# Expert loop and recurrences of a fused two-layer block: third pair of banks, scaled sums, later exponentials

## The reference

```
ek, ekv = exp(min(f, 30)), exp(min(f, 30)) * f
a[t] = a[t-1] * decay + ekv[t]          # forward, and once more from the end backward
b[t] = b[t-1] * decay + ek[t]
euk  = exp(min(u + f, 30))
num  = a_fwd + a_bwd - ekv + euk * f
den  = b_fwd + b_bwd - ek + euk
out  = sigmoid(x) * num / max(den, 1e-8) * (0.8 + 0.2 tf)
layer 0: x = x + MoE(attention(out))    # 16 heads, 8 experts, top 2, FF = 896
layer 1: x = x + fp8_mlp(out')          # weights and rows rounded to e4m3, 704 inner channels
```

## Time and profile before

| | us |
|---|---|
| median of three runs (648.53 to 650.09) | 648.83 |
| the profiled execution | 650.63 |
| its span, first to last instruction | 648.5 |

### The profile page before, as it was taken

The page is one execution under the profiler, slowest core; times in us unless marked ns, Lnnn a source line. Parts: engine busy times, 40 slices in busy tenths (PEclk is TensorE's granted clock), DMA queues, the critical chain, the costliest instruction groups (busy, mean ns, idle before and its releaser), DMA issues.

```text
span 648.5 us, 10885 instructions
## 1 busy us (share of the span) xinstructions
PE 503.3 (78%) x3862; PEld 411.0 (63%) x3862; DVE 518.6 (80%) x973; ACT 359.1 (55%) x760; POOL 262.1 (40%) x212
## 2 busy tenths in 40 slices
PE   2011198599999999998578997979988999666775
PEld 1000043278888878887458896979978999533453
DVE  4999868688888888885528958998889889579993
ACT  3226235687777778775115545645455456447671
POOL 3565114754444445530554279361362140070011
PEclk9999999989999999999579999999998999978797
DMA  8300004050000000000278796779875764030001
GB/s 269 118 0 1 1 1 129 0 172 2 1 2 3 1 2 10 25 1 3 77 252 327 273 312 142 259 269 254 294 285 166 285 147 132 27 103 25 9 25 33
DMA packets 36529, 71.85 MB, mean 111 GB/s; under 512 B 5276, under 2 KB 21916, under 8 KB 36220
## 3 DMA queue, kind: packets, MB, share of 16 engines
q10 hardware_dynamic: 16912, 46.27, 21.0%
q1 hardware_dynamic: 16491, 16.75, 8.1%
q0 software_dynamic: 3072, 8.14, 5.2%
HBM read 66.03 MB, written 5.12 MB: 110 GB/s over the span
## 4 chain that ended last, share of the span: by engine, by line
PE 49%; DVE 32%; issue 7%; ACT 6%; POOL 2%; DMA 1%; ACTq 0%; DVEq 0%; SPq 0%; POOLq 0%; PEldq 0%
PE pw L418 8%; PE pb L418 8%; PE pb L609 7%; PE sc L609 6%; PE sc L459 6%; PE po L418 4%; PE pt L470 3%; DVE areg L1168 2%; DVE areg L1154 2%; DVE areg L1152 2%; DVE rs L1566 1%; DVE areg L1513 1%; DVE areg L1165 1%; DVE areg L1506 1%; DVE breg L1225 1%
## 5 line engine op out<-in xcount | busy, mean ns | idle before, releaser
L609 PE MATMUL pb<-areg,wreg 128*128 128x128 f32 x736 | 86.3, 275 | 6.1 <-DVE areg L1506 3.8
L609 PEld LDWEIGHTS pb<-areg,wreg 128*128 128x128 f32 x736 | 84.0, 192 | 7.2 <-issue 5.2
L609 PE MATMUL sc<-areg,wreg 128*128 128x128 f32 x552 | 67.5, 280 | 8.7 <-DVE areg L1506 8.7
L1711 POOL TENSOR_TENSOR breg<-breg,con 128x512 f32<-128x512 f32 x32 | 40.7, 1271 | 80.9 <-ACT breg L846 80.9
L609 PEld LDWEIGHTS sc<-areg,wreg 128*128 128x128 f32 x552 | 65.3, 196 | 9.5 <-DVE areg L1506 9.5
L418 PE MATMUL pb<-areg,wreg 128*128 128x512 f16 x240 | 58.9, 382 | 2.0 <-ACT breg L846 1.9
L980 ACT CAST areg<-areg 128x512 f16<-128x512 f32 (+1 forms) x46 | 25.8, 561 | 62.5 <-DVE areg L1506 56.0
L418 PE MATMUL pw<-areg 128*128 128x256 f16 x406 | 56.5, 273 | 1.6 <-DVE areg L1520 1.6
L854 ACT ACTIVATE breg<-breg,mx 128x128 f32<-128x128 f32 (+1 forms) x128 | 56.6, 445 | 2.0 <-DVE mx L1276 1.9
L459 PE MATMUL sc<-areg,breg 128*128 128x128 f32 (+1 forms) x256 | 48.0, 331 | 6.4 <-DVE mx L1276 5.2
L1520 DVE TENSOR_TENSOR areg<-areg 128x512 f16<-128x512 f32 (+1 forms) x46 | 39.8, 866 | 14.0 <-ACT areg L980 13.7
(11 more groups left out here) (245 smaller groups left out, 1246.7 us busy)
## 6 DMA issues: line engine op xcount, KB each, us to landing
wreg<-in_L_ffn_w ACTq DMA_DIRECT2D x46, 896.0 KB, 7.3
wreg<-in_L_ffn_w SPq DMA_DIRECT2D x8, 896.0 KB, 7.8
ys_dram<-areg ACTq DMA_DIRECT2D x23, 128.0 KB
wreg<-in_L_ffn_wq SPq DMA_DIRECT2D x1, 2048.0 KB, 8.6
wreg<-in_L_ffn_wo SPq DMA_DIRECT2D x1, 2048.0 KB, 8.1
areg<-in_fside_BxSxS ACTq DMA_DIRECT2D x4, 256.0 KB, 5.5
x_in<-in_x SPq DMA_DIRECT2D x4, 256.0 KB, 4.0
h_dram<-areg SPq DMA_DIRECT2D x8, 128.0 KB, 1.7
```

Source lines behind the costliest of these rows:

```text
L609: last = nc.tensor.matmul(bank[:, j * P:(j + 1) * P], up_w[n % SLOTS_UP][:, m, c, at:at + P], xsT[:, parity, c * P:(c + 1) * P], start=c = ...
L1711: G.tensor_tensor(t2[:, parity, :].rearrange("p (b n) -> p b n", b=2), t2[:, parity, :].rearrange("p (b n) -> p b n", b=2), rope_sin.rearr ...
```

## The change

1. Up products use three pairs of banks in turn, `pb2`, `sc2`, `pt2`: part p of tile n takes pair (2n + p) mod 3 and waits for the product of the part three before.
2. Backward states of the next step, times the decay, are added to the forward states: bwd[t+1] * decay equals bwd[t] less the input of t. So the input need not be subtracted, and GpSimd's subtraction (L1694) goes, with the link before it. The sum becomes two scalar-tensor-tensor instructions, one for each half of the channels.
3. The exponentials of the second recurrence come at tiles 1, 6, 9 and 15, before at 0, 5, 8 and 14.
4. The up weights of tiles 0 to 2 are loaded by SyncE, those of tiles 1 and 2 when the first gather has landed; before, ScalarE issued them, 1 and 2 behind its copy of x of tile 0.
5. VectorE takes the product of part 1 before the low half of part 0.
6. GpSimd's four residual sums are spread: one behind each gather of tiles 18 and 19, two ahead of the first folding.

```diff
+        def load_up(eng, n):
+            k = n % SLOTS_UP
+            if n >= SLOTS_UP:
+                eng.wait_ge(s["upb_done"], n - SLOTS_UP + 1)
+            e = eng.value_load(tmi[0:1, n:n + 1], min_val=0, max_val=NE - 1)
+            for m, name in enumerate(("L0_ffn_w1", "L0_ffn_w3")):
+                eng.dma_start(up_w[k][:, m], t[name][bass.ds(e, 1)].rearrange("e (c p) n -> p (e c) n", p=P)).then_inc(s_u[k], 16)
...
+            sp.wait_ge(s["wo_done"], 2)
+            sp.wait_ge(s["tmi_ready"], 1)
+            load_up(sp, 0)
+            sp.wait_ge(s_xs[0], 16)
+            load_up(sp, 1)
+            load_up(sp, 2)
             sp.wait_ge(s["tmap_ready"], 1)
...
+        def up_pair(n, part):
+            return (pb2, sc2, pt2)[(2 * n + part) % 3]
...
             def up(n, parity, part):
                 first, count = (0, FA // P) if part == 0 else (FA // P, FB // P)
+                before = 2 * n + part - 3
+                if before >= 0:
+                    pe.wait_ge(s["inner_b_done" if before % 2 else "inner_a_done"], before // 2 + 1)
                 for m in range(2):
-                    bank = pb[m] if part == 0 else sc2[:, m]
+                    bank = up_pair(n, part)[:, m, :]
...
-                    if n >= 1:
-                        pe.wait_ge(s["inner_a_done"], n)
                     up(n, parity, 0)
...
-                    if n >= 1:
-                        pe.wait_ge(s["inner_b_done"], n)
                     up(n, parity, 1)
...
-            act.wait_ge(s["wo_done"], 2)
-            act.wait_ge(s["tmi_ready"], 1)
-            load_up(0)
             act.wait_ge(s["tmap_ready"], 1)
             act.wait_ge(s["h2_out"], 16 * NT)
             copy_xT(0, 0)
-            load_up(1)
-            load_up(2)
...
-            exponentials_at = {0: 0, 5: 1, 8: 2, 14: 3}
+            exponentials_at = {1: 0, 6: 1, 9: 2, 15: 3}
...
+            def add_later_states(l, b, fwd, bwd):
+                for c in range(C):
+                    lo, hi = c * S, (c + 1) * S
+                    last = V.scalar_tensor_tensor(fwd[:, :, lo:hi - 1], bwd[:, :, lo + 1:hi], decay[:, l, c, b:b + 1],
+                                                  fwd[:, :, lo:hi - 1], ALU.mult, ALU.add)
+                return last
...
-                link(V.tensor_tensor(fwd[:, :, :], fwd[:, :, :], bwd[:, :, :], ALU.add))
+                link(add_later_states(0, b, fwd, bwd))
...
-                    link(V.tensor_tensor(fwd[:, :, :], fwd[:, :, :], bwd[:, :, :], ALU.add))
+                    link(add_later_states(1, b, fwd, bwd))
...
+                silu(n, 1)
                 inner_low(n, n % 2, 0)
-                silu(n, 1)
                 w2_low(n, n % 2)
...
-                link(G.tensor_tensor(U[:, 0, :], U[:, 1, :], fT[:, b, :], ALU.mult))
-                G.tensor_tensor(U, U, E, ALU.subtract).then_inc(s["u_ready"], 1)
+                G.tensor_tensor(U[:, 0, :], U[:, 1, :], fT[:, b, :], ALU.mult).then_inc(s["u_ready"], 1)
...
             load_scales(0, 2 * INTER)
             gather_tiles(18)
-            for b in range(B):
-                last = G.tensor_tensor(x0[:, TT * b:TT * (b + 1), :].rearrange("p i n -> p (i n)"),
-                                       x0[:, TT * b:TT * (b + 1), :].rearrange("p i n -> p (i n)"), x_in[:, b, :], ALU.add)
-            last.then_inc(s["xsum_ready"], 1)
-            gather_tiles(19, 20)
+            add_residual(0)
+            gather_tiles(19)
+            add_residual(1)
+            gather_tiles(20)
             pool.wait_ge(s["rq_ready"], 3)
             pool.wait_ge(s["rq_copied"], 2)
             pool.wait_ge(s["scale_in"], 16)
+            add_residual(2)
+            add_residual(3).then_inc(s["xsum_ready"], 1)
             fold_scales(0)
```

More of the change, by code:

```diff
@@ L1001, in _ @@
                         act.wait_ge(s["inner_low"], 2 * n - 1)
-                    nc.scalar.activation(inner[:, 0:FA], pb[0][:, :], ACT.Silu).then_inc(s["silu_a_done"], 1)
+                    nc.scalar.activation(inner[:, 0:FA], up_pair(n, 0)[:, 0, :], ACT.Silu).then_inc(s["silu_a_done"], 1)
                 if n + 1 < MT:
@@ L1013, in _ @@
                         act.wait_ge(s["inner_low"], 2 * n)
-                    nc.scalar.activation(inner[:, FA:FF], sc2[:, 0, 0:FB], ACT.Silu).then_inc(s["silu_b_done"], 1)
+                    nc.scalar.activation(inner[:, FA:FF], up_pair(n, 1)[:, 0, 0:FB], ACT.Silu).then_inc(s["silu_b_done"], 1)
                     if n + SLOTS_UP < MT:
-                        load_up(n + SLOTS_UP)
+                        load_up(act, n + SLOTS_UP)
                     inner_high(n, parity, 1)
@@ L1503, in silu @@
                 lo, hi = (0, FA) if part == 0 else (FA, FF)
-                bank = pb[1][:, 0:FA] if part == 0 else sc2[:, 1, 0:FB]
+                bank = up_pair(n, part)[:, 1, 0:hi - lo]
                 dve.wait_ge(s["silu_a_done" if part == 0 else "silu_b_done"], n + 1)
@@ L1780, in _, with add_residual @@
             recurrence_inputs(1, 3)
+            def add_residual(b):
+                return G.tensor_tensor(x0[:, TT * b:TT * (b + 1), :].rearrange("p i n -> p (i n)"),
+                                       x0[:, TT * b:TT * (b + 1), :].rearrange("p i n -> p (i n)"), x_in[:, b, :], ALU.add)
             def load_scales(lo, hi):
```

## The result

| | before | after |
|---|---|---|
| median, us | 649.46 (648.53 to 650.78, 4 runs) | 638.43 (637.43 to 640.37, 4 runs) |
| the profiled execution, us | 650.63 | 639.25 |
| its span, us | 648.5 | 637.4 |
| from the start to the first projection | 86.69 | 82.19 |
| from there to the first up product | 247.77 | 246.69 |

The ratio is 0.984, with a 95% interval of 0.980 to 0.987. The kernel is 11.0 us faster; 20.1 us were forecast, and 638.4 lies outside the range of 624.5 to 636.5. The table of stages says where to look: the first stage gave the 4.5 us that it was to give, the loop gave 5.05 of 15.6, so 10.6 us are missing there.

What follows compares the result with a forecast made beforehand. The expert loop was taken as bound by TensorE, its idle time the prize. First stage 4.5 plus loop 15.6 made 20.1 us less, forecast 628.7 us, own range 625.5 to 631.5, wider range 624.5 to 636.5.

Steps and rivals of the forecast that it cites:

- Part 1: First recurrence: dropping GpSimd's subtraction saves 5.3 us, two scaled sums cost 0.8 us, so 4.5 us less.
- the rival of half the rate: VectorE's scaled sums run at half rate, 2.6 us a pair, 1.2 more in each of four batches: 633 us; chance 0.05.
- on another victim: First stage, batch 0: GpSimd's remaining product still delays some other VectorE instruction, a toll of about 1 us.
- Part 3: Expert loop: three bank pairs and the new order end bank waits, 12.5 us together; rounding gives 1.5, tile 15's clock 1.9.
- Part 2: Loop: later exponentials end SiLU's lateness; tile 8's gather goes out near 395.6, takes 4.0 us, wanted near 401.
- cover of 1.5 us: Tile 8: the forecast margin, some 1.5 us, between the gather's landing and TensorE wanting its rows.
- The fourth rival: GpSimd, waiting longer at the exponentials, sends gathers late at tiles 8, 12, 18; TensorE stands, up to 656 us; chance 0.03.
- The second rival: Banks do nothing: ScalarE's copy of x holds up products as long; 8.7 us of waits stay, 638 us; chance 0.08.
- The end of the loop: Behind the last tile the new order leaves SiLU's lateness unhidden: a loss of 0.4 us.
- Part 4: Loop: GpSimd's split residual sums still hold VectorE somewhat; TensorE loses 0.5 us, bounds 0 to 3.
- Part 5: Tile 1: weight load from SyncE goes out about 1.0 us sooner, VectorE's late rounding eats 0.4, gain 0.6 us.
- The first rival: VectorE becomes the loop's bound and loses 6 us over 14 tiles: 635 us; chance 0.20.

Runs made afterwards that it cites:

- run 8: Changed kernel with the scales sent behind the gathers, plus GpSimd's subtraction and VectorE's plain sum back in both layers: 635.21 us, ratio 0.979.
- run 1: Changed kernel with GpSimd's send of the first scales moved behind the gathers of tiles 8 to 11: 629.34 us, ratio 0.967.
- run 6: Changed kernel with the scales sent behind the gathers, plus the exponentials at their old tiles 0, 5, 8 and 14: 635.50 us, ratio 0.980.
- run 4: Kernel before the change with only the exponentials moved to tiles 1, 6, 9 and 15: 648.37 us, ratio 0.998.
- run 7: Changed kernel with the scales sent behind the gathers, plus up products on two pairs of banks again: 629.70 us, ratio 0.970.
- run 5: Changed kernel with the exponentials at old tiles 0, 5, 8 and 14, the send still ahead of the gathers: 636.79 us, ratio 0.979.
- run 9: Changed kernel with the scales sent behind the gathers, plus VectorE's low half of part 0 ahead of the product of part 1 again: 630.42 us.
- run 11: Changed kernel with the scales sent behind the gathers, plus four residual sums in one row ahead of the gathers of tiles 19 and 20: 626.50 us.
- run 12: Changed kernel with the scales sent behind the gathers, plus two pairs of banks and the residual sums in one row: 627.10 us, ratio 0.966.
- run 3: Changed kernel with the send in its place, but each partition's 8 scales written as one run of 32 bytes: 629.88 us, ratio 0.970.

## Why the prediction failed, point by point

**The bound of the loop** was read rightly: TensorE wherever nothing holds it. It ran tiles 10 to 15 without a break, at 8.96 and 8.76 us a tile.

**Part 1 held.** The forecast was 4.5 us for the first stage and 4.5 came between these two traces. Over all traces the first projection starts at 81.8 us on average with the edit (eleven kernels, 80.9 to 82.5) and at 85.9 without it (three, 85.4 to 86.7): 4.1 us, so the last decimal was luck. VectorE's rows of the first stage, which answer:

```profile
12.34 0.43 DVE L1132 TENSOR_SCALAR areg<-ratio 128x512 f32<-128x512 f32 x1
...
18.96 2.23 DVE L1155 SCALAR_TENSOR_TENSOR areg<-areg,decay 128x510 f32<-128x510 f32 x2
21.22 1.23 DVE L1178 TENSOR_TENSOR areg<-areg 128x1024 f32<-128x1024 f32 x1
...
42.08 0.42 DVE L1132 TENSOR_SCALAR areg<-ratio 128x512 f32<-128x512 f32 x1
...
49.87 1.44 DVE L1155 SCALAR_TENSOR_TENSOR areg<-areg,decay 128x510 f32<-128x510 f32 x2
```

The clamps fell from 2.51 and 2.57 to 0.43 and 0.42 us, the sum with U from 3.26 to 1.23. A pair of scaled sums takes 1.44 us where 1.42 was taken, so the rival of half the rate, and with it the rule of the Trainium skill's Vector Engine (DVE) Microarchitecture Reference, section 7, "Points that are easy to get wrong", does not hold for this form: 2.6 us would have been its time, by the prediction's estimate. In batch 0 the pair took 2.23 us beside GpSimd's product, the toll "on another victim". In the loop the edit was counted inside part 3; run 8 gives it 3.3 us there.

**Part 2 is the step that failed**, in its last sentences. The place was right, tile 8; so was the moment of the issue: 395.6 on the old scale was forecast, and 389.61 is 395.2 on it, since the loop began 5.6 us earlier. TensorE wanted the rows at 394.1, on the old scale 399.7 and not 401, which left 4.5 us and not 5.4. But the term that failed is "takes 4.0 us". That number came from the earlier trace rows, the issues of 320 to 346 us, where nothing of the kind runs beside the gather. The same view of the window in question gave 8.5 us, and its GB/s line showed a stretch of 8 us with few bytes. At the true 13.1 us the cover of 1.5 us becomes a lack of 8.6, and that is the stand. Without the send ahead of it the same gather takes 3.6 us (run 1), so 4.0 was a fair price for a gather alone: what the sum left out is the send. The fourth rival thus had the place and the kind of loss, with a chance of 0.03. It was discounted by GpSimd's idle time, which says nothing on how long a transfer takes once it is issued. It also asked for the gather to be sent late; it was enough that TensorE came early.

The size could have been read before the change: that very gather took 10.1 us there, and with it the same sum gives a stand of some 5 us.

The other half of part 2 was too modest: it booked 2.8 us and 1.0 us of waits for banks as the price of the early exponentials. Run 6 gives them 6.2 us of the time and 8.5 of the loop, and run 4 shows that the wait of 1.97 us at 397.6 was theirs as well.

**Part 3: right amount, owner in part wrong.** 12.5 us of bank waits did go (there is none in the waits after). The prediction gave the waits at 391.6 and 421.9 us to part 2 and the rest to the banks, since ScalarE's copy of x had long been made in those stands. That showed that a third pair could remove them, not that nothing else would: in run 4 they are all gone without it, though the three later ones behind a stand of 9.84 us, and run 7 found nothing lost without it. The second rival, "the banks do nothing", was therefore right in its title and wrong in its price of 8.7 us. The 2.8 us for rounded weights all went, and not 1.5. The prediction read them as one place, tile 2; they are two waits, 1.06 us at 368.1 (tile 3) and 1.75 us at 432.3 (tile 9), and both are back with the early exponentials (runs 5 and 6). The lower clock of tile 15 went, 1.9 us as reckoned, but 1.25 us for a lower clock came behind the new stand and 1.1 at the end of the loop (granted 0.83 from 545 to 552 us). The second doesn't follow from the wait alone: in run 1 the same 3.44 us are followed by the last products at a granted clock of 1.00, in 2.47 us.

**The end of the loop** was to cost 0.4 us. It cost 2.9: the last down product (which answers the tile of the earlier trace rows) waits 3.44 us for VectorE against 1.64, and its 21 products take 3.56 us against 2.47. The new order, for which the 0.4 us stood, is not the cause (run 9), and the row of 544.85 below shows VectorE waiting for ScalarE before it.

```profile
543.09 0.68 DVE L1519 TENSOR_TENSOR areg<-areg,pt 128x512 f32<-128x512 f32 x1
544.85 0.55 DVE L1519 TENSOR_TENSOR areg<-areg,pb 128x384 f32<-128x384 f32 x1 [1.07 <-ACT areg L1019]
...
548.46 3.56 PE L437 MATMUL pw<-areg 128*128 128x256 f16 x21 [3.44 <-DVE areg L1533]
```

**Part 4** put 0.5 us for the spread sums, with bounds 0 and 3. TensorE felt nothing at tiles 15 and 18, where they run, though VectorE was held at tile 18, for 4.70 and 3.92 us, where 2.02 and 0.66 are usual. It was held by the two foldings (from 507.30 and 513.41 us), which come 2.5 us later for the two sums ahead of them:

```profile
507.84 4.70 DVE L1526 SCALAR_TENSOR_TENSOR areg<-wreg,areg 128x1792 f16<-128x1792 f16 x1
512.46 0.55 DVE L1533 TENSOR_TENSOR areg<-areg 128x384 f16<-128x384 f32 x1
512.93 3.92 DVE L1450 TENSOR_TENSOR_SCAN areg<-decay,areg 128x256 f32<-128x256 f32 x1
```

It shows later, as up to 1.5 us of the wait at the loop's end (run 11); that the lateness is carried there from tile 18 is argued, not shown, and with two pairs of banks the difference is 0.25 us (runs 7 and 12). At tile 15 the spreading saved at most the 1.38 us of run 12.

**Part 5** was to give 0.6 us; the wait for the weights of tile 1 fell from 1.64 to 1.45, so 0.2. Over all traces it is 1.3 us on average with the edit (twelve kernels, 1.06 to 1.69) and 1.64 and 1.71 in the two without. This edit was not undone by itself.

**The sum.** With the slow send out of the way the whole gain is 20.1 us of the median (649.4 to 629.3) and the loop's 16.5, against forecasts of 20.1 and 15.6. That agreement is partly one of errors that cancel: too much for the banks, too little for the exponentials and the rounding, too little for the end. What failed is one term, the transfer at tile 8, worth 9.9 us by the trace and 9.1 by run 1. Nor does the range follow from its parts: first stage 3.0 to 5.5 and splitting 0 to 3 give 627.2 to 632.7, and not 625.5 to 631.5; the measured time lies outside either. The first rival, VectorE as the bound, is not seen: TensorE had 44.79 of 44.79 us in tiles 10 to 14, with VectorE at 40.28.

**What stays open.** Taken out last, the exponentials are worth 6.2 us, the subtraction 5.9, and the banks, the order and the spreading nothing or less. Before and run 6 differ by 8.0 us of loop, of which the subtraction is 3.3 by run 8; how the other 4.7 are shared among SyncE's loads, banks and order, where the early exponentials are in place, was not tried. The middle stage is 1.1 us shorter after; over the other traces it lies between 245.9 and 247.2, so I put that down to spread.

## What to carry to other kernels

Where an edit makes an engine arrive sooner, look up everything that it will then ask for in the window in which it will ask, and take the duration of a transfer from there, never from a quiet stretch. A slice in which the DMA engines are busy and move few bytes costs nothing until an engine waits for a transfer in it; look for a transfer of single words behind it, write it in runs, or send it behind what is urgent. And several waits on different resources may have one cause: before a resource is added for each, remove the cause alone and see what is left.

## What the runs showed of the hardware

704 words of 4 bytes, 2.8 KB, hold up the transfers of both queues that have work for 6 to 8 us. The first gather behind them lands in 13.1 us, and in 3.6 with the words sent later (run 1); the two weight transfers on ScalarE's queue in 11.7 and 15.1 us instead of 4.9 and 8.2. The same bytes as 88 runs of 32 land in 1.9 us, the gather behind them in 5.9 and those weights in 4.5 and 7.8 (run 3).

GpSimd instructions with two inputs in SBUF, run back to back, hold one VectorE instruction for the whole row of them and not for one: 5.70 us beside four of 1.23 (run 12), as 5.89 before the change. The Trainium skill's SBUF — State Buffer, "Who interferes with whom", says that a VectorE instruction with two SBUF inputs contends with a GpSimd instruction that reads SBUF. The trace agrees, and adds that VectorE did not get in between the four instructions either.
